# Keys of the second group issued from ScalarE's queue, and that group's first scores ahead of three butterfly products

## What is computed

```python
x = x + window_attention(layernorm(x))   # 16 heads of 8, 2 key/value heads, window 32
x = x + ffn(layernorm(x))
x = x + linear_attention(layernorm(x))   # phi(q), phi(k) with phi = elu + 1
x = x + ffn(layernorm(x))
```

## Time and profile before

| what | us |
|---|---|
| median of 3 runs | 546.55 (546.40 to 546.69) |
| the profiled execution | 546.01 |
| its span | 544.2 |
| TensorE (PE) busy | 516.2 (95%) |
| GpSimd (POOL) busy | 448.7 (82%) |
| VectorE (DVE) busy | 425.8 (78%) |
| ScalarE (ACT) busy | 356.3 (65%) |

### The profile page before, as it was taken

How to read it: one execution, slowest core, us unless ns; L and a number is a source line. 1 busy time by engine, 2 the same in 40 slices (tenths; PEclk the granted TensorE clock), 3 DMA queues, 4 the chain that set the end, 5 groups by cost and what they waited for, 6 DMA issues and landing times.

```text
span 544.2 us, 14354 instructions
## 1 busy us (share of the span) xinstructions
PE 516.2 (95%) x5060; PEld 339.7 (62%) x5060; DVE 425.8 (78%) x1273; ACT 356.3 (65%) x578; POOL 448.7 (82%) x640
## 2 busy tenths in 40 slices
PE   4778888999999999999999999999999999999997
PEld 2454344746657666667667676666676676767765
DVE  5879788998878888787888888888879777844441
ACT  1654447576767677676778777776777777746552
POOL 7538889999989999899899989999989787797241
PEclk9999999999999999999999999999999999999999
DMA  8433323232322313142423223131431312010001
GB/s 304 148 97 91 95 62 87 62 84 51 90 57 51 90 38 84 37 108 47 104 50 91 48 61 83 43 94 45 119 73 42 88 27 64 21 40 20 1 20 40
DMA packets 49559, 38.87 MB, mean 71 GB/s; under 512 B 12368, under 2 KB 38992, under 8 KB 49488
## 3 DMA queue, kind: packets, MB, share of 16 engines
q1 hardware_dynamic: 47040, 33.73, 24.8%
q10 hardware_dynamic: 2448, 4.22, 2.1%
HBM read 15.64 MB, written 5.51 MB: 39 GB/s over the span
## 4 chain that ended last, share of the span: by engine, by line
PE 70%; POOL 15%; issue 4%; DMA 3%; DVE 3%; SPq 2%; ACT 2%; POOLq 0%; DVEq 0%; ACTq 0%
PE ring L807 17%; PE ring L785 16%; PE ps_s L753 8%; PE ring L727 7%; POOL probs_t L614 6%; PE ps_o L770 4%; PE ring L818 4%; PE ring L838 4%; PE ring L888 2%; PE ring L827 2%; PE ring L865 2%; DMA probs_t<-probs_t 1%; POOL xn_P L568 1%; POOL xb_W L584 1%; DMA x_P<-in_x 1%
## 5 line engine op out<-in xcount | busy, mean ns | idle before, releaser
L614 POOL TENSOR_TENSOR probs_t<-probs_t,first 128x1024 f32<-128x1024 f32 x64 | 151.1, 2369 | 19.3 <-DMA probs_t<-probs_t 19.3
L807 PEld LDWEIGHTS ring<-w,early 128*128 128x128 f32 x1024 | 119.1, 192 | 10.0 <-issue 9.0
L1211 ACT ACTIVATE early<-ring,b 128x512 f32<-128x512 f32 x128 | 84.3, 685 | 62.0 <-PE ring L785 61.6
L807 PE MATMUL ring<-w,early 128*128 128x128 f32 x1024 | 119.9, 275 | 1.2 <-ACT early L1211 1.1
L1202 ACT ACT_TABLE_LOAD x58 | 74.4, 1283 | 10.8 <-issue 9.8
L1220 ACT ACTIVATE probs_t<-merged_t 128x1024 f32<-128x1024 f32 x64 | 65.8, 1044 | 11.1 <-DVE merged_t L1579 8.9
L753 PE MATMUL ps_s<-kx,q_t 64*32 64x512 f32 x960 | 64.7, 596 | 2.5 <-DMA kx<-kv_rows 1.6
L1587 DVE STREAM_TRANSPOSE ps_o<-ps_o 128x512 f32<-128x512 f32 x64 | 46.2, 721 | 21.0 <-PE ps_o L770 21.0
L785 PE MATMUL ring<-xT_G,w1b 128*128 128x512 f32 x128 | 60.9, 595 | 0.7 <-ACT xT_G L1192 0.7
L785 PE MATMUL ring<-xT_F,w1b 128*128 128x512 f32 x128 | 60.1, 608 | 0.4 <-ACT xT_F L1192 0.3
L1560 DVE COPY_PREDICATED ps_s<-first,ps_s 128x512 f32<-128x512 uint32 x64 | 44.0, 687 | 17.2 <-PE ps_s L753 16.1
(11 more groups left out here) (126 smaller groups left out, 990.2 us busy)
## 6 DMA issues: line engine op xcount, KB each, us to landing
probs_t<-probs_t SPq DMA_DIRECT2D x256, 64.0 KB, 2.0
kx<-kv_rows SPq DMA_DIRECT2D x120, 40.0 KB, 2.2
x_P<-in_x SPq DMA_DIRECT2D x16, 256.0 KB, 3.1
out_x<-x_G SPq DMA_DIRECT2D x15, 256.0 KB, 2.5
vx_t<-kv_rows SPq DMA_DIRECT2D x128, 8.0 KB
up_s<-in_up_m ACTq DMA_DIRECT2D x7, 256.0 KB, 7.5
down_s<-in_down_m ACTq DMA_DIRECT2D x7, 256.0 KB, 7.5
kv_rows<-kv_t SPq DMA_DIRECT2D x16, 80.0 KB, 2.7
```

Of the source, the lines that this page charges most:

```text
L614: nc.gpsimd.tensor_tensor(parts, parts, keep.rearrange("p (a t) -> p a t", a=1).to_broadcast([P, PAIR * HEADS, WIN]), ALU.mult).then_inc(p ...
L807: last = nc.tensor.matmul(sums[:, P * j:P * (j + 1)], hid[s][:, c, P * j:P * (j + 1)], w2[:, c], start=(c == chunks[0]), stop=(c == chunks ...
L1211: nc.scalar.activation(hid[s][:, c], bank(name)[:], ACT.Gelu, bias=b1[:, c:c + 1]).then_inc(drained[BANK[name]].sem, 1)
```

## The change

ScalarE gets a `spread_keys` of its own, for group 1 alone: it waits for the stored keys and for the cleared tile, and issues the eight DMAs on ScalarE's queue, behind the copy of X.u3a and ahead of the copy of q. SyncE's queue no longer issues them. On ScalarE, `probs_out(0, 1)` moves ahead of the copies of X.d1 and X.u4a. On TensorE, `scores(1, 0)` moves ahead of X.d2, X.u5a and X.u5b, and the table `PRODUCTS` counts it so.

```diff
-    ("X.u4b", 0, "2", 0, 0), ("X.d2", 0, "0", 0, 0), ("X.u5a", 0, "3", 0, 0), ("X.u5b", 0, "2", 0, 0),
-    ("W.S0", -1, "S", 1, 1), ("X.u6b", 0, "2", 0, 0), ("X.d3", 0, "3", 0, 0), ("X.u6a", 0, "0", 0, 0),
+    ("X.u4b", 0, "2", 0, 0), ("W.S0", -1, "S", 1, 1), ("X.d2", 0, "0", 0, 0), ("X.u5a", 0, "3", 0, 0), ("X.u5b", 0, "2", 0, 0),
+    ("X.u6b", 0, "2", 0, 0), ("X.d3", 0, "3", 0, 0), ("X.u6a", 0, "0", 0, 0),
...
             def spread_keys(g):
 
                 sp.wait_ge(kv_out.sem, kv_out.after(g, "P.ko"))
-
-                if g == 1:
-                    sp.wait_ge(kx_cleared, 1)
-                else:
-                    sp.wait_ge(product.sem, product.after(g - 1, *SCORES))
+                sp.wait_ge(product.sem, product.after(g - 1, *SCORES))
...
                 if t == 0:
-                    spread_keys(1)
                     spread_probs(0, 1)
...
                     up_stage(4, "b")
+                    scores(1, 0)
                     down_stage(2)
                     up_stage(5, "a")
                     up_stage(5, "b")
-                    scores(1, 0)
                     up_stage(6, "b")
...
+            def spread_keys(g):
+
+                act.wait_ge(kv_out.sem, kv_out.after(g, "P.ko"))
+                act.wait_ge(kx_cleared, 1)
+                for h in range(HPK):
+                    act.dma_start(kx[h:P:HPK, h].rearrange("d (j n) -> d j n", j=TILES), keys_of(g)
+                                 ).then_inc(kx_in.sem, 16)
...
                     up_stage_out(3, "a")
+                    spread_keys(1)
                     attention_q_out(1)
+                    probs_out(0, 1)
                     down_stage_out(1)
                     up_stage_out(4, "a")
-                    probs_out(0, 1)
                     up_stage_out(4, "b")
```

## The result

| | median us | executions |
|---|---|---|
| before | 546.56 | 544.57 to 548.06 |
| the change | 550.47 | 549.47 to 553.20 |

The ratio is 1.0084, with a 95% interval of 1.006 to 1.0108: the change is slower by 3.3 to 5.9 us. The sign was forecast, but the size wasn't: 548.0 was predicted, and the range ended at 549.5. The profiled execution of the change took 549.78 us (span 548.0). One execution of the kernel before, in the later runs, took 1324 us; it belongs to the slow runs and is left out of all ratios.

What follows compares the result with a forecast made beforehand. It took the chain through scores(1, 3) and group 2's keys, then a full TensorE, to bound the kernel. 0 for the keys' wait plus 1.5 us of delay on 546.55 gave 548.0 us, range 546.6 to 549.5.

Steps and rivals of the forecast that it cites:

- The sign: Whole kernel: slower by more than the 1.1 us that a measurement can tell from no change, chance 0.64.
- What bounds, and the path: Chain from 42 to 58 us: scores(1, 3) release group 2's keys; a 1.5 us lag there reaches the full TensorE stretch.
- the keys' wait: TensorE's 0.49 us wait for group 1's keys before scores(1, 0): removed by the change, gain 0 on the ending chain.
- the lag is made up: Rival: unseen slack between 58 and 105 us absorbs the delay; 546.7 us, chance 0.08.
- The order on TensorE and ScalarE: Products and copies behind scores(1, 0) come later, so scores(1, 1) start at 43.0, 1.6 us late.
- landing took at most 1.64 us: Group 1's key store, issued at 26.57, has landed by 28.2, so ScalarE's key issues can start at 28.7.
- A TensorE idle for some tenths more: Extra TensorE idle time before X.u4b and X.d3 costs nothing more while the granted clock stays at 1.00.
- fit into the gap: Rival: ScalarE's key issues take 0.45 us each and it is free by 33.0; 547.2 us, chance 0.16.
- the queues hinder each other: Rival: ScalarE's key issues wait for SyncE's until 30.46, 1.8 us later; 549.8 us, chance 0.06.
- Faster by a shifted long issue: Rival: SyncE's long issue in group 2's keys shifts and 1.1 us leave the chain; 545.4 us, chance 0.12.
- the exponential's place: On ScalarE, the exponential ahead of X.d1 makes X.d1 1.8 us late, X.u4b 36.0 not 34.99, and buys nothing.

Runs made afterwards that it cites:

- e3: The change with ScalarE's exponential put back behind the copies of X.d1 and X.u4a; median 548.38 us, 1.0034 to 1.0076 against the kernel before.
- e4: The change plus two unread 128x512 matmuls in TensorE's idle stretch ahead of X.u4b; 1.0037 to 1.0082 against the kernel before.
- e1: The kernel before with only TensorE's order changed, scores(1, 0) ahead of X.d2, X.u5a and X.u5b; 1.0067 to 1.0114 against the kernel before.
- r_filler: The change plus two unread matmuls ahead of X.u4b, run again beside the change itself; median 548.92 us, 1.0053 to 1.0084 against the kernel before.
- e2: The kernel before with only group 1's key issues moved to ScalarE's queue; 1.0016 to 1.0057 against the kernel before.
- b2: The kernel before with probabilities (0, 0) ahead of group 1's key store, its value issues on ScalarE, a third start matmul; ratio 0.9967, again 0.9957.
- r_after: The change run again unaltered, beside the change with fillers; median 550.68 us, 1.0077 to 1.0132 against the kernel before.
- b1: The kernel before with probabilities (0, 0) ahead of group 1's key store and its value issues on ScalarE; 544.58 against 545.67 us, 0.9979 to 1.0008.

## Why the prediction was right about the sign and wrong about the size

**What bounds, and the path** were right for the change. Nothing is gained by sooner scores(1, 0); the keys' wait was on no ending chain; the lag of scores(1, 3) goes on undiminished (4.8 us there, 4.9 still at the scores of group 7 to 11, and 5.9 at the last scores of all). For a smaller lag it isn't as sure: in the profiles of e3 and e4, which were 1.8 us late at scores(1, 3), near the 1.5 that I forecast, 0.6 were left at scores(3, 0). So the rival "the lag is made up" had something in it, though the times of e3 are 1.9 to 4.1 us above before.

**The order on TensorE and ScalarE** was right to 0.13 us: from scores(1, 0) to (1, 1) I had 6.45 us (36.55 to 43.0); e1, e3, e4 and r_filler, all at full clock in this stretch, measured 6.58 each. Before it was 3.40.

**The first step that failed** is "landing took at most 1.64 us; that of group 1, issued at 26.57, has then landed by 28.2". It is a term that I took from the store of group 0. In the eight profiles of the table the landing of group 1's store took 3.4 (before), 3.4, 3.7, 2.9, 3.8, 2.9, 1.6 and 3.6 us. In the change the key issues began at d = 0.08 in place of -1.18, 1.3 us late. The eight then took 5.32 us in place of 5.1, and 0.2 more was lost in small pieces up to the scores. So scores(1, 0) stood at d = 8.37, where the prediction's 36.55 is 6.67 (36.55 - 29.88): **1.7 us** more, most of it from the landing. The trace of before had the number: it could have been asked for that one store. A wait that nobody feels doesn't show in the views of waits, but it does when the waiting is moved to a queue that has something behind it.

**The second** is "A TensorE idle for some tenths more ... costs nothing more as long as the granted clock stays at 1.00". I named the condition and gave it no price and no chance. The idle stretch became 2.5 us and the clock didn't stay: 8.08 us in place of 6.58 from scores(1, 0) to (1, 1), **1.5 us**. All twelve executions of the change had a low mean clock. The first error lengthened the idle stretch from about 0.9 to 2.5 us, and so it probably brought on the second too; no run has the change with an early landing and without fillers.

The sum by these steps: 1.5 as predicted, 1.7 from the landing and the issues, 1.5 from the clock, 4.7 in all, against 4.79 in the trace and 3.3 to 5.9 in the times. Both failed terms added to a loss that was forecast without them, so the sign wasn't luck.

**The rivals.** The issues didn't fit into the gap: they took 0.62 us each on ScalarE's queue, not 0.45. Nor did the queues hinder each other by 1.8 us: in e4 they issued side by side, and the longest key issue in the change, beside SyncE's load of x, took 0.80 in place of 0.62. Faster by a shifted long issue: the long one in the keys of group 2 did become a little shorter, 1.43 in place of 1.68, and (2, 0) is 4.46 late and not 4.79; that is a third of a microsecond, not 1.1. Of the trade itself, the exponential's place cost about 1 us and was the part that earned nothing.

## What to carry to other kernels

Before DMA issues are moved to a compute engine's queue, ask the trace when their own precondition was met, for that very transfer, and not only how long the issues take: the whole queue stands for both. A new idle stretch on TensorE can have two prices, the wait and slower products behind it; here two matmuls that nobody reads, put into the stretch, took the second price away in both profiles that had them. And a move off a queue pays only where the chain passes through that queue at that time.

## What the runs showed that I hadn't expected

- The granted clock differs between executions of the same kernel: 20 of 68 executions of the kernel before, run beside the experiments, had a mean below 0.998, and 12 of 12 of the change. The length of the idle stretch alone doesn't decide. Stretches of 2.52 and 2.99 us had a low clock behind them; of the fourteen of 1.93 to 2.28 us in the twelve profiles, three had it (e2, b2 run again, and e4 2 us later); in r_after it came a second time, at 120 to 125 us, behind one of 1.62 us.
- How much a low clock costs the whole execution isn't the same everywhere. In the three sets of executions of the kernel before, those with a low mean had a median span of 544.8, 543.6 and 545.0 us, the others 543.8, 543.9 and 544.6.
- The landing of one and the same 80 KB store lay between 1.6 and 3.8 us in different executions, and 2.7 and 1.8 where the probabilities were issued ahead of it (b1, b2). What lengthens it stays open; no run took the DMAs behind it away. In every other profile with these DMAs behind the store one of the four issues took 1.1 to 1.9 us in place of 0.6, and the landing 2.9 us or more; in e4, where the store landed after 1.6 us, none did. Which is cause and which effect isn't shown.
- The kernel's scatter of 2 to 3 us has at least three sources in the traces: the slow or quick start (1.6 us), that landing, and low clocks at other places. Between scores(4, 1) and (4, 3) some profiles gained another 0.4 to 3 us of lag (most in r_after, with its second low clock), which wasn't followed up.
